# A fused delta-rule, MLP, attention and mixture kernel: output sum kept in PSUM, every engine's order of a head step refilled, fourth norm moved into attention

## The reference, cut to what matters

```python
x = x + gated_delta(layernorm(x))      # 16 key heads, 32 value heads of 128
x = x + mlp(layernorm(x))              # 256 -> 512 -> 512 -> 256, relu
y = layernorm(x); x = x + attention(y) # 4 heads of 64, softmax
y = layernorm(x)                       # the fourth norm
x = inp + experts(rmsnorm(inp) * w_norm) + shared(...)   # inp = x + y, 32 experts, top 4
```

```python
state = state * exp(g_t)
kv    = k_t @ state
delta = (v_t - kv) * b_t
state = state + outer(k_t, delta)
out   = q_t @ state
o     = o * silu(z); o = o * rsqrt(mean(o * o) + EPS) * gamma; y = o @ w_out
```

## Time and profile before

| | us |
|---|---|
| median of 3 runs (1553.78 to 1560.2) | 1554.52 |
| the profiled execution's own time | 1565.12 |
| its span in the trace | 1563.3 |
| PE busy in the span | 1346.6 (86%) |
| DVE busy | 1024.9 (66%) |
| ACT busy | 778.6 (50%) |
| POOL busy | 751.7 (48%) |

### The profile page before, as it was taken

One profiled execution on the slowest core, in us unless ns is written; L12 is line 12 of the kernel. 1 busy time (PEld: TensorE's weight loads), 2 busy tenths in 40 slices (PEclk: granted clock), 3 DMA queues, 4 the chain that ended last, 5 costly groups with the idle time before them and its releaser, 6 DMA issues. The chain is left out here.

```text
span 1563.3 us, 24959 instructions
## 1 busy us (share of the span) xinstructions
PE 1346.6 (86%) x8680; PEld 908.1 (58%) x8680; DVE 1024.9 (66%) x1958; ACT 778.6 (50%) x1915; POOL 751.7 (48%) x1226
## 2 busy tenths in 40 slices
PE   6687988989898898988989898899797799697994
PEld 3365655666565566656666665666545356453673
DVE  6865877787786877878787786966522266541354
ACT  3454756566565655646566564765432265210121
POOL 1774674756658476664756648572100000025263
PEclk9878989889998999989989998999999899889997
DMA  3513335343543535345343543545300870112387
GB/s 92 141 32 101 85 119 128 88 114 85 161 103 101 122 88 141 92 127 133 88 117 93 150 109 98 119 121 161 106 1 1 324 191 1 61 53 100 71 187 187
DMA packets 233181, 171.72 MB, mean 110 GB/s; under 512 B 163746, under 2 KB 202998, under 8 KB 230240
## 3 DMA queue, kind: packets, MB, share of 16 engines
q1 hardware_dynamic: 226912, 161.59, 37.8%
q0 software_dynamic: 6144, 8.53, 3.0%
HBM read 104.64 MB, written 65.83 MB: 109 GB/s over the span
## 5 line engine op out<-in xcount | busy, mean ns | idle before, releaser
L803 PE MATMUL psum_banks<-main_hT,gdn_w_in 128*128 128x512 f32 x512 | 247.1, 608 | 16.5 <-DVE heads_y L1286 10.4
L1286 DVE SCALAR_TENSOR_TENSOR heads_y<-psum_banks,gdn_conv_w,heads_y 128x1021 f32<-128x1021 f32 (+2 forms) x192 | 245.1, 1277 | 9.8 <-ACT heads_y L1099 4.8
L1579 POOL TENSOR_TENSOR heads_XT<-heads_XT,heads_tmp 128x126 f32<-128x126 f32 (+22 forms) x496 | 201.2, 406 | 38.9
L1576 POOL TENSOR_TENSOR heads_tmp<-heads_XT,heads_A 128x126 f32<-128x126 f32 (+22 forms) x496 | 191.9, 387 | 43.6 <-PE psum_banks L968 4.0
L803 PEld LDWEIGHTS psum_banks<-main_hT,gdn_w_in 128*128 128x128 f32 x512 | 93.8, 193 | 97.3 <-issue 77.1
L917 PE MATMUL psum_banks<-heads_w_z,main_hT 128*128 128x256 f32 x512 | 146.6, 438 | 0.0
L832 PE MATMUL psum_banks<-heads_S,heads_kT 128*128 128x256 f32 x224 | 77.3, 429 | 67.9 <-DVE heads_S L1307 66.1
L1561 POOL TENSOR_TENSOR heads_v_s<-heads_v_s,heads_k_root 128x2048 f32<-128x2048 f32 x16 | 58.2, 3638 | 158.4 <-DMA heads_v_s<-values_by_tokens 158.4
L1307 DVE SCALAR_TENSOR_TENSOR heads_S<-heads_S,heads_coef,psum_banks 128x128 f32<-128x128 f32 x192 | 57.2, 339 | 98.6 <-PE psum_banks L857 98.2
L917 PEld LDWEIGHTS psum_banks<-heads_w_z,main_hT 128*128 128x128 f32 x512 | 108.7, 223 | 21.8 <-issue 6.2
L2120 POOL DMA_INDIRECT expert_rows<-moe_rows,route_dest x32 | 31.4, 980 | 185.8 <-DVE route_dest L2099 176.3
(11 more groups left out here) (280 smaller groups left out, 3048.2 us busy)
## 6 DMA issues: line engine op xcount, KB each, us to landing
values_by_tokens<-heads_v_s SPq DMA_DIRECT2D x64, 256.0 KB, 4.1
heads_v_s<-values_by_tokens SPq DMA_DIRECT2D x16, 1024.0 KB, 5.7
outputs_by_features<-heads_ogT SPq DMA_DIRECT2D x120, 128.0 KB, 3.8
heads_ogT<-outputs_by_features SPq DMA_DIRECT2D x30, 512.0 KB, 4.1
main_w_gu<-in_w_gu SPq DMA_DIRECT2D x4, 2816.0 KB, 20.8
gdn_w_in<-in_w_in SPq DMA_DIRECT2D x16, 512.0 KB, 4.5
heads_A<-kk_blocks SPq DMA_DIRECT2D x64, 128.0 KB, 4.9
keys_by_tokens<-heads_k_tok SPq DMA_DIRECT2D x64, 128.0 KB, 3.2
```

Of the source, the lines that this page charges most:

```text
L803: ins = pe.matmul(out[:, half * 512:(half + 1) * 512], w_in[:, kd_, j * P:(j + 1) * P], hT[:, kd_, half * 512:(half + 1) * 512], start=kd_ ...
L1286: dve.scalar_tensor_tensor(y[j][:, shift:T], src[:, 0:T - shift], conv_w[:, head, j, t:t + 1], y[j][:, shift:T], ALU.mult, ALU.add).then_i ...
L1576: pool.tensor_tensor(tmp[:, 0:n, 0:m], bc_last(XT[:, 0:n, j], m), bc_mid(A0[:, j, j + 1:BLK], n), ALU.mult).then_inc(solve_step.sem, 1)
L1579: pool.tensor_tensor(XT[:, 0:n, j + 1:BLK], XT[:, 0:n, j + 1:BLK], tmp[:, 0:n, 0:m], ALU.add).then_inc(solve_step.sem, 1)
```

## The change

Four things are changed.

1. **The output sum.** DVE adds `O1` to the product in PSUM in place, and the gate's multiplication reads PSUM and writes `og`; for chunk 0 there is no copy any more. The semaphore `b_free`, which lets PE write that bank again, is raised by the multiplication instead of the sum, and ACT's squares wait for it too.
2. **The block scales.** `nd` is written by ACT (a new item `diagonal`, ahead of `norms`), DVE keeps the reciprocal and the transpose, and POOL forms `cb` itself. Head 0 stays as it was.
3. **The orders.** PE, ACT, DVE, SP and POOL tables of a step are filled anew.
4. **The fourth norm** runs in attention's last block, two token tiles at a time on ACT, DVE and POOL. The loads of the router's and shared weights move to the start of the routing block. The 97 semaphores of the head steps are cleared by POOL during attention's projections, 22 remain in the clearing block, and attention's own are not cleared.

```diff
 PE_PLAN = banked(rows("""
-0: z0/0 p0/-1
-1: p1/-1
+0: z0/0
+1: p0/-1 p1/-1
 3: z1/1
-4: norm_q/0 z2/2
+4: z2/2 norm_q/3
 5: p2/-1
 6: decay0/3 decay1/2 decay2/0 decay3/1
-7: kk0/3 p3/-1
-8: kk1/3
-9: attn0/1
-10: p4/-1 attn1/2
-11: y6a/3 y6b/0
-12: p5/-1
-13: u6a/3 u6b/0
-15: z3/1
-16: y7_0/0 p6/-1
-17: p7/-1
+7: p3/-1 kk0/3
+8: attn0/1 kk1/3
+9: attn1/2
+10: y6a/3 y6b/0
+12: p4/-1
+13: p5/-1 u6a/3 u6b/0
+14: z3/1
+16: y7_0/0 p6/-1 p7/-1
...
 DVE_PLAN = rows("""
...
-8: decay3 tap10
-9: tap11 tap12 turn
-11: attn0 ot0
-12: attn1 scales
-14: tap20 tap21
-15: tap22 ot1
+8: tap10 tap11 tap12 factors turn
+11: ot0 attn0
+13: scales tap20
+14: tap21 tap22 attn1
+15: ot1
...
-                    if c == 0:
-                        dve.tensor_copy(mine, bank_b[:, 0:2]).then_inc(b_free.sem, 1)
-                    else:
-                        dve.tensor_tensor(mine, bank_b[:, 0:2], O1[:], ALU.add).then_inc(b_free.sem, 1)
-                    dve.wait_ge(b_free.sem, b_free.done(h, f"o{c}"))
-                    dve.tensor_tensor(mine, mine, gate, ALU.mult).then_inc(og_ready.sem, 1)
+                    if c:
+                        dve.tensor_tensor(bank_b[:, 0:2], bank_b[:, 0:2], O1[:], ALU.add).then_inc(o_summed.sem, 1)
+                        dve.wait_ge(o_summed.sem, o_summed.done(h, f"o{c}"))
+                    dve.tensor_tensor(mine, bank_b[:, 0:2], gate, ALU.mult).then_inc(b_free.sem, 1)
...
+            def block_diagonal(h):
+                act.wait_ge(blk_loaded.sem, blk_loaded.end(h) * 16)
+                act.wait_ge(cb_step.sem, cb_step.base(h))
+                act.activation(nd[:], flat(A0[:])[:, 0:BLK * BLK:BLK + 1], ACT.Copy, bias=EPS, scale=-1.0).then_inc(cb_step.sem, 1)
...
             def eliminate(h):
-                pool.wait_ge(cb_step.sem, cb_step.done(h, "cb"))
+                if h:
+                    pool.wait_ge(cb_step.sem, cb_step.done(h, "rnd"))
+                    pool.tensor_tensor(cb[:], rnd[:], beta_rows[:, h], ALU.mult).then_inc(cb_ready.sem, 1)
...
+                for u in range(3):
+                    statistics(u)
+                    shifts(u)
+                    if u:
+                        scaled(u - 1)
                 feats_out(BLOCKS - 1)
+                scaled(2)
+                statistics(3)
+                shifts(3)
+                scaled(3)
```

More of the change, by code:

```diff
@@ L144, in _ @@
             act.activation(root[:], spread[:], ACT.Sqrt).then_inc(s_root, 1)
-            if rms:
-                act.wait_ge(s_spread, 2)
-                act.activation(root[:], spread[:], ACT.Sqrt).then_inc(s_root, 1)
         @block.tensor
@@ L280 @@
 ACT_PLAN = rows("""
-0: q_silu z0 q_square
-1: base0
-3: v0_silu
-4: v1_silu keys z1 z2
-7: exp0 gamma kk0 base1 exp1 exp2
-8: kk1
-9: exp3
-10: y6a
+1: q_silu z0 q_square v0_silu base0
+4: v1_silu z1 z2
+6: keys base1
+7: kk0 exp0 kk1 exp1
+10: exp2 exp3 gamma
+11: y6a
 12: y6b
-13: base2 u6a norms
+13: base2 diagonal norms
+14: u6a
 15: u6b
 16: z3 y7_0
-18: base3 u7_0
-19: y7_1
-21: u7_1
+18: base3
+19: y7_1 u7_0
+20: u7_1
 """)
@@ L305 @@
 7: exp0 exp1 exp2 exp3 base3
-11: norms
+11: diagonal norms
 13: y6a y6b
@@ L375, in belongs @@
         return h in FINISH and h <= HK
-    if name.startswith(("kk", "p", "solve", "base", "tap", "keys", "norms", "scales")):
+    if name.startswith(("kk", "p", "solve", "base", "tap", "keys", "norms", "diagonal", "scales")):
         return h in AHEAD
@@ L575, in heads @@
     dt_ready = per_head("dt_ready", *[f"dt{c}" for c in range(C - 1)], steps=SCAN)
[L576 removed]
+    o_summed = per_head("outputs_summed", *[f"o{c}" for c in range(1, C)], steps=SCAN)
     sq_ready = per_head("squares_summed", *[f"sq{c}{e}" for c in range(C) for e in range(HD)], steps=SCAN)
@@ L1130, in squares @@
             def squares(h, c):
-                act.wait_ge(og_ready.sem, og_ready.done(h, f"og{c}"))
+                act.wait_ge(b_free.sem, b_free.done(h, f"o{c}"))
                 if c == 0 and h in FINISH:
@@ L1816, in _ @@
                 outputs(3)
+                for half in range(2):
+                    if half == 0:
+                        for i in range(2):
+                            pe.wait_ge(s_pt[i], 2 * R)
+                    else:
+                        pe.wait_ge(s_add, 2)
+                    for t in range(4 * half, 4 * half + 4):
+                        pe.wait_ge(s_xn, t + 1)
+                        for kd in range(KD):
+                            ins = pe.transpose(turn_bank[half][kd][:, t % 4], rows[:, t, kd * P:(kd + 1) * P], ident[:])
+                    ins.then_inc(s_turned, 1)
             @block.scalar
```

203 lines of the change are left out of this document (132 added, 71 removed).

## The result

The changed kernel takes 1463.52 us, median of 4 runs (1461.61 to 1466.12), against 1556.33 us before (4 runs); the ratio is 0.9403 with a 95% interval of 0.9376 to 0.943. The forecast was 1471 us in a range of 1450 to 1525. The profiled execution has a span of 1464.3 us.

The account below looks back on a forecast made before the run. PE, busy 86% of the span, was taken as the bound, so only its idle or half-clock time could be won. Terms -73 - 5 - 7 + 1 = -84 gave 1481 from the profiled 1565.12, 1471 us against the median; range 1450 to 1525.

Parts of the forecast that it names:

- the half clock: PE running at half clock behind its wait for the new state; removing it was to gain 3.6 us a step.
- The new state ahead of the scales: DVE's order in a head step: 4.1 us of PE waiting plus 3.6 of half clock gained, 7.7 a step.
- ACT's order: ACT's queue before the fourth chunk's Dl: PE waits 1.7 us there, 1.2 a step more than before.
- Block scales split: Scales shared by ACT, DVE and POOL; reciprocal perhaps held beside POOL's v_s scaling: +0.7 us a step, bounds 0 to 1.5.
- Output sum in PSUM: DVE's gates in a step shorten to 416 ns, little gained on the path; b_free later: +0.2 us a step.
- Clearing: Before attention's first product: 98 fewer semaphore clears there, -7 us.
- Fourth norm: Attention's end to routing: norm under attention -1.5 us, router weights landing later +2.5, together +1; bounds -8 to +8.
- the first rival: Head steps: the half clock stays behind the new wait before L851, 47 us come back, 1518 us; chance 0.17.
- the second rival: Head steps: late blocks hold ACT's diagonal, so PE waits for Dl instead; about 1543 us; chance 0.10.
- the slower case: Head steps: blocks land over 3 us later against the scan, total over 1554.5 us; chance 0.04.

Follow-up runs that it names:

- the second execution of the kernel before: The kernel before, unchanged, profiled a second time: 1563.12 us in one run, a step 66.86 us.
- the run with growing waits: The changed kernel with extra small ACT copies ahead of the fourth chunk's Dl, one more each step from step 3: 1482.51 us in one run.
- the run with both edits: The kernel before with block scales behind the fifth chunk's new state on DVE and the output sum in PSUM: 1514.38 us, ratio 0.97.
- The run that mends both: The changed kernel with DVE's last softmax rows ahead of the norm's first shifts and router weights loaded during attention: 1455.01 us, ratio 0.9342.

## Why the prediction was right

**Time and place.** The forecast sum, -84, stands against -92.8 in the medians and -91.4 in the spans without the accident of the last stretch. Of the full steps' -6.38 us for the -5.6 forecast, the state's wait is -4.0, the half clock -2.7, the waits for `Dl` +1.4, the taps ahead of the projections -0.75 and X -0.3. I had set -84 against a profiled execution 10.6 us above its median and carried the offset over; that was right, as most of its surplus lay in a part that the change does not touch.

**The new state ahead of the scales:** right. The wait for the state went from 4.14 to 0.14 us a step. The half clock, in every step before, stayed in two of the 13. Its going gave 2.7 us a step, not 3.6 (784.5 to 749.7 us busy), or 2.3 by the second execution of the kernel before.

**ACT's order:** right in place and cause, 1.24 us for the 1.7 forecast, 0.76 more than before and not 1.2. Its price was less than its length, too: in the run with growing waits the first 0.2 to 0.3 us more cost nothing, and shortening it by 0.52 gained nothing, because DVE's queue sets the next state there.

**Block scales split:** the size was right (0.70 us before the sixth chunk's L824), the cause wrong. I expected POOL to hold the reciprocal; it takes 0.35 us in every step, in step 2 in the middle of POOL's product, so it is no instruction that POOL holds. What PE waits for is ACT's own row: diagonal, norms (0.59 us of waiting for DVE's transpose before them), `O1` and two copies. What I did not see was the other half, that the diagonal's read had to leave DVE: back there, it costs 11 to 14 us, 0.7 a step.

**Output sum in PSUM: the term that was wrong.** I had the gate right (423 ns for the 416 forecast, from 629) and its value wrong: "on the path it gives little", +0.2 a step in the sum. Alone it gains 29 us, and without it the changed kernel loses 15 to 17, 0.9 a step. I had averaged the gate over the step; what counts is the one gate beside POOL with X behind it. In the kernel before it is the fifth chunk's, 1.73 us in every step and 0.55 of PE's waiting; in the new order it would be the fourth chunk's, 1.31 us beside the scaling of `og` and 1.16 of waiting.

**The order alone: too large, and the sum in part luck.** The 7.7 a step that I gave to it belong to several edits together. By itself the order gave 3.1 a step (66.84 to 63.71), because the stall moved to X, and with the sum in PSUM no more than that in the profile (63.73). Undone in the changed kernel (60.47) it costs 1.8 a step, the output sum 0.9, the diagonal on DVE 0.7. The 3.3 a step between the run with both edits and the changed kernel come from the diagonal and from the other orders together. The traces show what the other orders do here: the blocks' load lands 33.0 us into a step with both edits (steps 2 to 13, on average), where PE comes to the sixth chunk at 31.7, and 31.1 in the changed kernel, where PE comes at 32.7. So the load was late for the scan and is now early, and a held read costs less. Which item of the new orders brings the load forward no run shows. The sum came out because what I gave to one move in excess, the parts that I put at nothing or at a cost made up for.

**Not in the sum:** 0.75 us a step before the projections, which waited for taps (9.7 us in 13 steps before, 0 after); step 1, -7.6 for -4; step 15, +1.5 for -1; and +2.3 in attention, where the clock is at the half from 1150.5 to 1157.4 as well (0.51). Why it falls there was not tested.

**Clearing:** PE's wait is 3.33 us for 10.27, -6.9 against -7.

**Fourth norm:** right, +1.6 for +1. The last output came 11.8 us behind ACT's inverse, which is 1361 on the time scale before, as forecast, and PE waited 2.92 us for the router's weights where 1.26 are left without them, 1.7 for the 2.5 forecast. The run that mends both gets 7.5 us from the same stretch, which this part of the change, as made, left lying.

**The rivals:** the half clock that the first rival feared behind the new wait came in two of the 13 steps, 2.2 us in all and not 47. That is no rule for waits of 1.24 us: the same wait left the clock alone in the other eleven. The blocks held ACT for 0.45 us in step 2 and in no later step; they came 1.7 us earlier in a step than before, where the second rival had them as late. It and the slower case had no part.

## What to carry to other kernels

Before an instruction is moved out of a wait, ask what will stand in the same moment beside the long operation of the other engine: here POOL's 3.6 us held the diagonal's read, then in some steps the gate, then the read again, and the four products ahead of them would have held another gate. Look at every step, too, not at one: with the output sum undone the gate that took 3.06 us cost PE 0.49 us, and in most steps its like cost nothing, while one of 1.31 us cost 1.16 in each. Test an edit alone and undone: 37, 29 and 44 us for two edits and both, and 15 to 17 for one of them undone, told what the total could not. And a wait that is shortened on one queue gains only if the next queue is not already as late; read that queue first.
